# Causal attention of 64-key blocks: scores of 1280 columns a step, two value layouts in one slot, and a mask by GpSimd's product

## What is computed

```
x = x + long_convolution(layernorm(x))
x = x + experts(layernorm(x))          # 8 experts, hidden 256, top 2
x = x + attention(layernorm(x))        # 16 heads of 8, 4 query sets, one key and value set
x = x + experts(layernorm(x))

# attention, for each query set g:
att = q @ k.T / sqrt(8);  att = where(causal, att, -inf);  y = softmax(att) @ v
out = concat(y over the 4 sets) @ W_proj.T
```

## Time and profile before

| what | value |
|---|---|
| time before, median of 3 runs | 804.67 us (804.52 to 804.86) |
| the profiled execution, from its first to its last instruction (span) | 802.7 us |
| what lies around the span, if the profiled execution took the median | 804.67 - 802.7 = 1.97 us |
| busy in the span: TensorE, ScalarE, VectorE, GpSimd | 760.7, 721.1, 652.5, 560.4 us |
| instructions | 20426 |

### The profile page before, as it was taken

The page is one execution under the profiler, slowest core; times in us unless marked ns, Lnnn a source line. Parts: engine busy times, 40 slices in busy tenths (PEclk is TensorE's granted clock), DMA queues, the critical chain, the costliest instruction groups (busy, mean ns, idle before and its releaser), DMA issues.

```text
span 802.7 us, 20426 instructions
## 1 busy us (share of the span) xinstructions
PE 760.7 (95%) x7674; PEld 414.0 (52%) x7674; DVE 652.5 (81%) x1917; ACT 721.1 (90%) x932; POOL 560.4 (70%) x685
## 2 busy tenths in 40 slices
PE   5888999999999999999999999999989999999996
PEld 4345666677775333333333333333334777677774
DVE  7998999999876677778787777787566898989885
ACT  5918999999999999999999999999997999899984
POOL 2898665655436988888988888888896545445442
PEclk9999999999999999999999999999999999999998
DMA  9210000000044343443453334424400000000000
GB/s 276 67 64 29 1 2 2 2 2 2 8 100 106 80 93 88 98 83 90 105 107 96 90 91 90 98 67 106 107 1 2 1 15 16 15 14 16 15 15 18
DMA packets 37962, 45.70 MB, mean 57 GB/s; under 512 B 6137, under 2 KB 23810, under 8 KB 37858
## 3 DMA queue, kind: packets, MB, share of 16 engines
q1 hardware_dynamic: 37858, 44.33, 22.2%
HBM read 27.53 MB, written 16.78 MB: 55 GB/s over the span
## 4 chain that ended last, share of the span: by engine, by line
PE 54%; ACT 19%; DVE 14%; issue 11%; POOL 1%; DMA 0%; ACTq 0%; DVEq 0%; POOLq 0%
PE psum L1006 13%; ACT prob L1272 13%; PE psum L937 13%; PE psum L1316 12%; PE psum L1263 5%; DVE mixed L1025 4%; PE psum L1374 4%; ACT hidden_first L951 2%; ACT hidden_parts_first L953 2%; PE psum L1154 1%; PE psum L686 1%; DVE hidden_parts_first L960 1%; DVE hidden_parts_second L960 1%; DVE stats L362 1%; PE psum L646 1%
## 5 line engine op out<-in xcount | busy, mean ns | idle before, releaser
L1272 ACT ACTIVATE prob<-psum 128x1536 f32<-128x1536 f32 x256 | 347.6, 1499 | 14.4 <-PE psum L1263 14.4
L1279 POOL TENSOR_SCALAR_AFFINE_SELECT prob<-prob 128x512 f32<-128x512 f32 (+3 forms) x448 | 305.9, 712 | 41.1 <-ACT prob L1272 31.7
L1316 PE MATMUL psum<-prob,vstack 128*32 128x256 f32 (+1 forms) x2048 | 204.9, 495 | 1.6 <-DVE o_tok L1324 1.6
L937 PE MATMUL psum<-xt_parts,w_parts 128*128 128x512 f16 x768 | 186.6, 379 | 0.0
L1025 DVE SCALAR_TENSOR_TENSOR mixed<-psum,comb_y,mixed 128x128 f32<-128x128 f32 x512 | 143.2, 340 | 1.5 <-PE psum L1006 1.5
L967 POOL TENSOR_TENSOR hidden_parts_second<-hidden_second,hidden_parts_second 128x512 f16<-128x512 f32 x64 | 77.4, 1209 | 93.5 <-ACT hidden_parts_second L953 93.5
L967 POOL TENSOR_TENSOR hidden_parts_first<-hidden_first,hidden_parts_first 128x512 f16<-128x512 f32 x64 | 77.6, 1213 | 78.1 <-ACT hidden_parts_first L953 78.1
L1263 PE MATMUL psum<-qstack,kstack 32*128 32x512 f16 x768 | 99.7, 385 | 9.2 <-ACT prob L1272 7.8
L1263 PEld LDWEIGHTS psum<-qstack,kstack 32*128 32x128 f16 x768 | 24.9, 91 | 157.3 <-ACT prob L1272 138.7
L937 PEld LDWEIGHTS psum<-xt_parts,w_parts 128*128 128x128 f16 x768 | 71.2, 98 | 64.1 <-issue 1.4
L951 ACT ACTIVATE hidden_second<-psum,b 128x512 f32<-128x512 f32 x128 | 88.4, 691 | 15.4 <-PE psum L937 12.0
(11 more groups left out here) (148 smaller groups left out, 848.4 us busy)
## 6 DMA issues: line engine op xcount, KB each, us to landing
qstack<-qk_parts SPq DMA_DIRECT2D x128, 128.0 KB, 3.5
qk_parts<-parts SPq DMA_DIRECT2D x64, 192.0 KB, 3.1
kstack<-qk_parts SPq DMA_DIRECT2D x128, 32.0 KB, 3.5
stream<-u_folded SPq DMA_DIRECT2D x4, 512.0 KB, 8.1
kept_x<-stream SPq DMA_DIRECT2D x4, 512.0 KB, 2.6
out<-mixed SPq DMA_DIRECT2D x7, 256.0 KB, 2.3
w_whole<-L_ffn_W SPq DMA_DIRECT2D x1, 1024.0 KB, 9.0
taps<-c_taps SPq DMA_DIRECT2D x1, 640.0 KB, 7.1
```

Source lines behind the costliest of these rows:

```text
L937: last = e.matmul(bank(u % 4), m.w1[:, w_part, ex, cols], xt_parts[:, s, x_part, :], start=(n == 0), stop=(n == len(PRODUCTS) - 1))
L1272: e.activation(prob[:, n % PROBS, :], psum[:, TILE * (n % 2):TILE * (n % 2 + 1)], ACT.Exp, scale=SCALE)\
L1279: return e.affine_select(kept, kept, [[0, kept.shape[1]], [0, 2], [sign, P]], ALU.is_ge, 0.0, base=0, channel_multiplier=-sign)
L1316: last = e.matmul(to[SLOT * lane:SLOT * (lane + 1)], vstack[:, b % 2, keys, first:first + SLOT], weights_of(n - t, lane, keys, pair), star ...
```

## The change

Keys are cut into blocks of 64. For one lane a step's first bank holds "full" scores (all first 128 keys against the last 128 queries, which need no mask). The second bank, of another lane, holds "early" keys: the first 64 of each half against that half's 128 queries, one half on partitions 0 to 63 and the other on 64 to 127. The last 256 columns, of a third lane, hold "late" keys: the second 64 of each half against its own 64 queries. That is 1280 columns a step, still four steps a quad. Scores are six matmuls of 64 columns width in place of three of 128. The mask is on columns 512 to 767 and 1024 to 1279 of every step, two `tensor_tensor` products on GpSimd with a constant tile `keep` of 128x64, read four times over. The weighted sums of a quad are three (full 512, early 512, late 256 columns). Two constants, `turn` (64 KB) and `keep` (32 KB), are loaded. The probability ring has 9 tiles. v takes 18 matmuls of half width in place of 6, and three copies in place of one. Projection takes 16 half-width matmuls a tile record in place of 8.

```diff
-TILE = 3 * BANK
-SUMS_Q = ((0, 0, 1), (1, 0, 2), (1, 1, 2), (0, 1, 3))
-PROBS = 7
+PART = P // 2
+EARLY, LATE, FULL = range(3)
+SUMS_Q = 3
+TILE = 2 * BANK + SETS * PART
+PROBS = 9
...
+        "c_turn": np.roll(np.eye(P, dtype=np.float32), -PART, axis=1),
+        "c_keep": np.where(np.concatenate([np.tri(PART).T, np.tri(PART)]) > 0, 1.0, 0.0).astype(np.float32),
...
-        vstack = sb("vstack", [P, 2, HALVES, 2 * HD + HEADS * SLOT], of=own)
+        vstack = sb("vstack", [P, 2, 3, HEADS * SLOT], of=own)
...
+        e.dma_start(turn[:], dr["c_turn"]).then_inc(s_attw, 16)
+        e.dma_start(keep[:], dr["c_keep"]).then_inc(s_attw, 16)
...
-            last = e.transpose(bank(at_bank(b))[:, h * P:(h + 1) * P], normed[:, HALVES * b + h, :], eye[:])
+            last = e.transpose(bank(at_bank(b))[:, h * P:(h + 1) * P], normed[:, HALVES * b + h, :], (eye, turn)[h][:])
...
-        for h in range(HALVES):
+        for kind in (EARLY, LATE, FULL):
             for i, (w_part, x_part) in enumerate(PRODUCTS):
-                last = e.matmul(bank(6)[:, h * P:(h + 1) * P], at_x[:, s, x_part, h * P:(h + 1) * P],
-                                wqkv_parts[:, w_part, SETS + 1, :], start=(i == 0), stop=(i == len(PRODUCTS) - 1))
+                for half in range(2):
+                    first = PART * (half if kind == FULL else 2 * half + kind)
+                    last = e.matmul(bank(6)[half * PART:(half + 1) * PART, kind * P:(kind + 1) * P],
+                                    at_x[:, s, x_part, first:first + PART], wqkv_parts[:, w_part, SETS + 1, :],
+                                    start=(i == 0), stop=(i == len(PRODUCTS) - 1))
...
+        full, both, late = to[:, 0:BANK], to[:, BANK:2 * BANK], to[:, 2 * BANK:TILE]
+        for half in range(2):
+            rows = slice(half * PART, (half + 1) * PART)
+            early_keys, late_keys = slice(half * P, half * P + PART), slice(half * P + PART, (half + 1) * P)
+            e.matmul(full[rows], kstack[lanes[0], s, c, rows], queries[0][:, 1], start=True, stop=True)
+            e.matmul(both[rows], kstack[lanes[1], s, c, early_keys], queries[1][:, half], start=True, stop=True)
+            last = e.matmul(late[rows], kstack[lanes[2], s, c, late_keys], queries[2][:, half, 1], start=True, stop=True)
...
     def scalar_exp(e, n):
         if n >= PROBS:
-            q, t = divmod(n - PROBS, 4)
-            e.wait_ge(weighed, 4 * q + (3 if t < 2 else 4))
+            e.wait_ge(weighed, SUMS_Q * ((n - PROBS) // 4 + 1))
...
     def gpsimd_mask(e, n):
+        bands = prob[:, n % PROBS, BANK:]
+        bands = [bands[:, at:at + SETS * PART].rearrange("p (g q) -> p g q", q=PART) for at in (0, BANK)]
+        kept = keep[:].rearrange("p (g q) -> p g q", g=1).to_broadcast([P, SETS, PART])
         e.wait_ge(exped, n + 1)
...
+        for band in bands:
+            last = e.tensor_tensor(band, band, kept, ALU.mult)
+        last.then_inc(masked, 1)
...
+    def tensor_weigh(e, q, i):
...
+        if kind == FULL:
+            e.wait_ge(exped, 4 * (q + 1))
         else:
+            e.wait_ge(masked, 4 * (q + 1))
...
-            last = e.matmul(project_bank(b)[:, h * P:(h + 1) * P], o_rows[:, g // 2, h, g % 2, :], wproj[:, g, :],
-                            start=(g == 0), stop=(g == SETS - 1))
+            for half in range(2):
+                last = e.matmul(project_bank(b)[half * PART:(half + 1) * PART, h * P:(h + 1) * P],
+                                o_rows[:, h, half ^ h, g, :], wproj[:, g, :], start=(g == 0), stop=(g == SETS - 1))
...
     def tensor_second(e):
-        tensor_weigh(e, LAST - 4)
-        tensor_weigh(e, LAST - 3)
+        tensor_weigh(e, LAST // 4 - 1, 0)
         e.wait_ge(exped, LAST)
         tensor_up(e, second, 0, 0)
-        tensor_weigh(e, LAST - 2)
+        tensor_weigh(e, LAST // 4 - 1, 1)
         tensor_up(e, second, 0, 1)
-        tensor_weigh(e, LAST - 1)
+        tensor_weigh(e, LAST // 4 - 1, 2)
...
-                at = n - n % 4 - 4
-                for i in ((), (0,), (1, 2), (3,))[n % 4]:
-                    tensor_weigh(e, at + i)
+            if n >= 4 and n % 4:
+                tensor_weigh(e, n // 4 - 1, n % 4 - 1)
```

More of the change, by code:

```diff
@@ L164, in build_in @@
     eye = sb("eye", [P, P])
+    turn, keep = sb("turn", [P, P]), sb("keep", [P, PART])
     in_bounds = sb("in_bounds", [P, P])
@@ L226, in build_in @@
         o_tok = sb("o_tok", [P, 2, BANK], of=own)
[L227 to L229 removed]
+        o_norm = sb("o_norm", [P, HALVES, 2 * 2 * SETS, SLOT], of=own)
+        rden = sb("rden", [P, 2, QUADS, 2 * 2 * SETS, HALVES], of=own)
+        o_rows = sb("o_rows", [P, HALVES, 2, SETS, PART], of=own)
     with ExitStack() as own:
@@ L1235, in vector_v, with lanes_of, score_banks @@
         if b >= 2:
-            e.wait_ge(weighed, STEPS_B * (b - 1))
-        e.tensor_scalar(v_places(b), v_source(), 1.0 / WSCALE, None, ALU.mult).then_inc(v_copied, 1)
+            e.wait_ge(weighed, SUMS_B * (b - 1))
+        for to, made in v_moves(b):
+            last = e.tensor_scalar(to, made, 1.0 / WSCALE, None, ALU.mult)
+        last.then_inc(v_copied, 1)
     def step_of(n):
         return n // STEPS_B, n // 4 % QUADS, n % 4
+    def lanes_of(t):
+        return t, (t + 1) % LANES, (t + 2) % LANES
+    def score_banks(n):
+        at = 3 * BANK * (n % 2)
+        return psum[:, at:at + TILE]
     def tensor_scores(e, n):
         b, c, t = step_of(n)
-        s, to = b % 2, psum[:, TILE * (n % 2):TILE * (n % 2 + 1)]
+        s, to = b % 2, score_banks(n)
         if n >= 2:
@@ L1256, in tensor_scores @@
             e.wait_ge(s_stack[s], STACK * (b // 2 + 1))
[L1257 to L1264, removed]
+        lanes = [slice(SLOT * lane, SLOT * (lane + 1)) for lane in lanes_of(t)]
+        queries = [qstack[at, s, c].rearrange("p g (h k q) -> p h k g q", h=HALVES, q=PART) for at in lanes]
+        full, both, late = to[:, 0:BANK], to[:, BANK:2 * BANK], to[:, 2 * BANK:TILE]
[5 more added lines that the diff above has]
+            last = e.matmul(late[rows], kstack[lanes[2], s, c, late_keys], queries[2][:, half, 1], start=True, stop=True)
         last.then_inc(scored, 1)
@@ new lines, in gpsimd_mask, with weights_of @@
+        last.then_inc(masked, 1)
+    def weights_of(n, lane, kind):
+        t = next(t for t in range(4) if lanes_of(t)[(FULL, EARLY, LATE).index(kind)] == lane)
+        at = {FULL: slice(0, BANK), EARLY: slice(BANK, 2 * BANK), LATE: slice(2 * BANK, TILE)}[kind]
+        return prob[:, (n + t) % PROBS, at]
+    def tensor_weigh(e, q, i):
+        b, c, _ = step_of(4 * q)
+        kind = (FULL, EARLY, LATE)[i]
+        if c == 0 and i == 0:
+            e.wait_ge(v_copied, b + 1)
+        if q == 0 and i == 0:
+            e.wait_ge(accum, EXPERTS * FFN_CHUNKS)
+        elif i == 0:
+            e.wait_ge(turned, q)
+        if kind == FULL:
+            e.wait_ge(exped, 4 * (q + 1))
+        else:
+            e.wait_ge(masked, 4 * (q + 1))
+        to = bank(7)[:, SETS * PART:BANK] if kind == LATE else bank(7)
@@ L1314, in tensor_weigh @@
         for lane in range(LANES):
-            first = SLOT * (c * LANES + lane) + 2 * HD * (1 - pair)
-            last = e.matmul(to[SLOT * lane:SLOT * (lane + 1)], vstack[:, b % 2, keys, first:first + SLOT],
-                            weights_of(n - t, lane, keys, pair), start=(t == 0), stop=(t == 3))
+            at = slice(SLOT * (c * LANES + lane), SLOT * (c * LANES + lane + 1))
+            last = e.matmul(to[SLOT * lane:SLOT * (lane + 1)], vstack[:, b % 2, kind, at], weights_of(4 * q, lane, kind),
+                            start=(i == 0), stop=(i == SUMS_Q - 1))
@@ L1632, in gpsimd_clear @@
         e.wait_ge(zeroed, 1)
-        ones = vstack[:, :, :, 2 * HD:].rearrange("p s h (n r) -> p s h n r", r=SLOT)
-        e.memset(ones[:, :, :, :, HD:HD + 1], 1.0).then_inc(zeroed, 1)
+        ones = vstack[:].rearrange("p s w (n r) -> p s w n r", r=SLOT)
+        e.memset(ones[0:PART, :, EARLY:FULL, :, HD:HD + 1], 1.0).then_inc(zeroed, 1)
+        e.memset(ones[PART:P, :, EARLY:FULL, :, UNIT + HD:UNIT + HD + 1], 1.0).then_inc(zeroed, 1)
+        e.wait_ge(zeroed, 3)
+        e.memset(ones[:, :, FULL, :, UNIT + HD:UNIT + HD + 1], 1.0).then_inc(zeroed, 1)
         e.memset(in_bounds[:], 1.0).then_inc(zeroed, 1)
```

53 lines of the change are left out of this document (20 added, 33 removed).

## The result

The changed kernel takes **832.14 us** (median of 4 runs, 827.10 to 837.14) where the kernel before takes 804.76 (4 runs). The ratio is 1.0336, 95% interval 1.0291 to 1.0382: slower, by 27.4 us. The forecast of 823.5 had the sign, its range of 803 to 846 holds the result, and it is 8.6 us short. The executions of the changed kernel lie further apart than those of the kernel before (804.52 to 804.92), and the longer ones have the lower mean granted clock of TensorE: 827.10 us at 0.986, 830.82 and 833.46 at 0.976, 837.14 at 0.968. That is a part of the answer, and the prediction had no word on it.

A forecast was written before the change was run, and what follows sets the result against it. GpSimd's mask products were to pace attention after the change: 20.1 us more there, 0.2 less at its start, 1.1 less behind the last mask, so +18.8 on 804.67 us gives 823.5 us, range 803 to 846.

The forecast's parts named there:

- Who bounds, and the change's work: In attention: GpSimd paces after the change, ScalarE leaves the bound with 294 us of exponentials, TensorE needs 20.6 us a batch.
- Rival 2: TensorE's scores: their halves follow each other, 0.54 us a step and 384 us in all, giving about 833 us; chance 0.14.
- The product: GpSimd's mask product of 256 columns takes 728 ns, 187 for the instruction plus 2.11 a column; 512 products take 351.2 us.
- rival 1: GpSimd's product is cheaper than forecast, under 0.649 us; at 0.585 or less TensorE paces, giving 776 us; chance 0.13.
- Rival 3: GpSimd's products don't overlap in attention: 0.728 us each, 21.5 us more, 845 us in all; chance 0.08.
- The stage: Attention takes 382.6 us for 362.46, 20.1 more: 351.2 products, 15.8 roots and low part, 0.6 start, 15 VectorE.
- VectorE's term: In attention, VectorE's operations beside GpSimd's products cost GpSimd 15 us (11 and 4), with bounds of 0 and 24 us.
- It fits, but closely: GpSimd runs without a break: TensorE's work in the fullest quad takes 5.7 us against 5.98 us of masks.
- The ends: Outside the attention stage: 0.2 us less at its start and 1.1 us less behind the last mask.
- its waits reach nobody: In attention, VectorE's waits beside GpSimd's products delay no other engine, as VectorE has 95 us to spare.
- Costed at nothing: Two loads, a larger clearing (1.2 us) and two more v copies (0.7 us a batch) are covered; uncovered copies cost 11 us.
- 95 us to spare: VectorE's free time in attention, taken to cover its waits and the added copies of v.

The follow-up runs named there:

- after_again: The changed kernel run again with nothing edited: 828.0 us (6 runs), ratio 1.0299 to the kernel before; its profiled execution took 825.52 us.
- act_norm: The changed kernel with 52 norms moved from VectorE to ScalarE: 826.41 us, ratio 1.0253 to the kernel before.
- one_product_act: The changed kernel with each step's two mask products joined into one and 52 norms moved to ScalarE: 801.89 us, ratio 0.9961 to the kernel before.

## Why the prediction was right, and where it wasn't

*Who bounds, and the change's work.* Right. ScalarE left the bound: 1.24 us an exponential (forecast 1.27) and 81.2 us idle (forecast some 80). Its busy time is 305.0 us and not the 294 of the forecast, which took over that neighbours overlap by 0.14 us (1499 ns for 1.36 us in the earlier trace rows); after it is 0.05 us. Off the bound this costs nothing. TensorE's six score matmuls in three row and two column strips start within 0.02 us, and the next group follows after 0.34 us, for 0.33 with three before; from the timeline of after:

```profile
409.56 0.40 PE L1279 MATMUL psum<-qstack,kstack 32*64 32x512 f16 x1
...
409.57 0.29 PE L1281 MATMUL psum<-qstack,kstack 32*64 32x256 f16 x1
409.90 1.06 PE L1323 MATMUL psum<-prob,vstack 128*32 128x512 f32 x8
```

Rival 2 (halves in turn, 0.54 us) falls with that, and the projection at full clock is still 1.09 us. By its own 0.54 us that rival had 23.8 us a batch and 381 us, not 24.0 and 384.

*The product.* Right to 1 ns: 727 for 728. So the line through 8 and 512 columns, taken together with the repeated 64-column tile, holds at 256, and rival 1 (under 0.649) falls. Rival 3 (no overlap) falls with the sum of the products: 363.0 us for 512 is 0.709 each, less than 0.727. In that page a group's busy time has the overlaps taken out. Without contention it would by estimate be 512 x (0.727 - 0.042) = 350.7, so VectorE's contention is some 12 us on the products, for the forecast's 15 of all.

*The stage.* An increase of 20.1 us was forecast; an execution with almost no half clock has +17.4 (379.85 us, `after_again`), the one shown first +26.3. The forecast's mechanism stands, 2.7 us too dear: the products with VectorE's term are 364.4 us for 366.2, and what lies beside them and the pauses is 14.3 us for 15.8. (The upper bound of VectorE's term comes to some 28 us by the prices given for it, 63 x 0.27 + 80 x 0.14, and not 24; nothing hung on it.) What is missing is in one sentence of it: "It fits, but closely". The 5.7 us of TensorE's fullest quad against 5.98 of masks were worked out at the granted clock of the earlier trace rows, where TensorE is 97% busy. The change itself takes that away: TensorE now waits for masks, in most batches 1.7 to 2.0 us at once. Then, at times, the clock goes to 1.2 GHz, projections take 1.81 for 1.09 us, and 0.28 us a quad in hand are not enough. **This is the step that failed**: TensorE's cost a quad was computed with a clock that was measured while TensorE was the bound. It is worth 8.9 us in the stage between two executions of the same kernel. Of the 8.6 us between forecast and result some 6.6 go with it, the way from the 825.52 us of `after_again` to the median of 832.14; the other 2 are what is left of two errors of opposite sign, as the sum below shows.

*The ends.* -1.1 us was forecast behind the last mask, +3.3 measured (`after_again`: 193.8 us from the last mask to the end, for 190.4 before); -0.2 at the start, +0.3 measured. The step that failed is "its waits reach nobody", said of VectorE. The timeline of `after_again` there:

```profile
626.50 3.45 POOL L1298 TENSOR_TENSOR prob<-prob,keep 128x256 f32<-128x256 f32 x5
...
627.87 1.47 DVE L380 TENSOR_SCALAR normed<-stream,meanvar,rstd 128x128 f32<-128x128 f32 x2
629.27 0.70 DVE L1331 STREAM_TRANSPOSE o_tok<-psum 128x512 f32<-128x512 f32 x1
...
630.02 1.59 PE L1323 MATMUL psum<-prob,vstack 128*32 128x512 f32 x8 [3.30 <-DVE o_tok L1331]
...
631.55 2.59 PE L937 MATMUL psum<-xt_parts,w_parts 128*128 128x512 f16 x6
...
637.16 0.72 DVE L1331 STREAM_TRANSPOSE o_tok<-psum 128x512 f32<-128x512 f32 x1 [2.08 <-PE psum L1323]
```

VectorE, beside back-to-back products, gets to the turn of the last quad but one only at 629.27. It is not the two norms alone: the six operations on 32 or 64 columns ahead of them (lines 856 to 870) take 3.4 us from start to start (624.44 to 627.87) where they took 1.7 before (606.74 to 608.42). The full sums, which need its bank, wait 3.30 us for it and start at 630.02, when the last mask (its end 629.94) is done already; and TensorE, after that wait, runs them and an up projection at half clock, 2.59 us where the next one takes 1.47. The last turn starts 7.2 us after the last mask instead of 3.2 (4.3 before). Of these 4.0 us some 1.6 are the half clock; the rest is that full sums and a second up projection now stand behind the last mask.

*The sum* for an execution like that, by its own numbers: 17.4 + 0.3 + 3.3 = 21.0 us, its span of 823.7 over 802.7. The forecast of 18.8 is this case less 2.2: +2.7 too much in the stage, 4.9 too little at the ends. That the forecast of 823.5 lies only 2 us from such an execution is in part luck, since the two errors have opposite signs. The rest up to the median of the first runs goes with the clock.

*Costed at nothing.* The loads, the clearing and the copies of v were not tried apart. `act_norm` took 52 norms from VectorE without a clear gain, which suggests that the 0.7 us a batch of copies had cover; it wasn't tried.

*Open.* Each half-clock stretch in attention of `after` begins in a wait of TensorE for masks or up to 1.0 us behind one, six times a wait of 1.7 to 2.0 us and once one of 2.9; but waits of the same length stand in other batches, and ten of them in `after_again`, without one. What decides it in a given batch was not found, nor whether the place of the added matmuls matters. What still paces `one_product_act`, 16.3 us of GpSimd's pauses, is open as well.

## What to carry to other kernels

Where an instruction has a fixed part of 187 ns beside 2.11 ns a column, cut a product into as few instructions as its layout allows: two bands in one instruction were worth some 14 us here, though VectorE's norms beside them then lasted up to 1.4 us. When a change moves the bound to another engine, recompute the costs of the one that loses it: a TensorE that begins to wait may not keep the clock at which its matmuls were measured, and can hand the loss back to the new bound. And an engine with "95 us to spare" has them only if its own operations keep their length beside the new neighbour.

## What was not expected of the hardware

- TensorE's granted clock fell to half inside a stage of steady work, at waits of 1.7 to 2.0 us (six times in one execution) and 2.9 us (once in it, and once in another that had ten of the shorter waits without it). The time of the kernel went with the clock: 825.52 us at 0.992, 837.14 at 0.968.
- Adding eight matmul records a batch, 16 us of work in all, made the kernel no slower and its times steadier: 824.83 to 826.40 us in five runs, against 825.52 to 837.14 in ten without them, six of which ran on another chip.
- VectorE's norm of 128 x 128 f32 mostly lasts until GpSimd's running product is over (all 52 in `after_again`): the 24 of `mixed` took 453 ns on average beside affine_selects, 727 beside products of 256 columns and 1275 beside products of 512. A bias on 4 columns took 481 ns beside products of 256 columns and 1066 beside products of 512 (`act_norm`, `one_product_act`).
